# Softmax tiles of the second attention: half of TensorE's transposes go to VectorE and DMA strips, and the k projections to another PSUM bank

## The reference

```python
q = (hidden_states @ Wq).reshape(B, S, H, dh)     # k and v alike
scores = jnp.einsum('bqhd,bkhd->bhqk', q, k) * scale + position_bias
probs = jax.nn.softmax(scores, axis=-1)
ctx = jnp.einsum('bhqk,bkhd->bqhd', probs, v).reshape(B, S, H * dh)
attn_output = ctx @ Wo
```

## Time and profile before

| | us |
|---|---|
| median of 3 runs | 1679.59 |
| lowest and highest | 1674.07, 1686.88 |
| the profiled execution | 1677.58 |
| its span | 1675.9 |
| busy in the span: PE, DVE, ACT, POOL | 1346.1, 879.9, 923.5, 522.0 |

### The profile page before, as it was taken

How to read it: one execution, slowest core, us unless ns; L and a number is a source line. 1 busy time by engine, 2 the same in 40 slices (tenths; PEclk the granted TensorE clock), 3 DMA queues, 4 the chain that set the end, 5 groups by cost and what they waited for, 6 DMA issues and landing times. The chain is left out here.

```text
span 1675.9 us, 22605 instructions
## 1 busy us (share of the span) xinstructions
PE 1346.1 (80%) x6711; PEld 596.6 (36%) x6711; DVE 879.9 (53%) x2700; ACT 923.5 (55%) x1844; POOL 522.0 (31%) x789
## 2 busy tenths in 40 slices
PE   2388988887629179999999999999999999997374
PEld 1123333332117023343343343343433433432253
DVE  2445556553311046657667657667577576674211
ACT  0277777776404047656666656666566666564031
POOL 4100222222224413233423433422433334224235
PEclk9699999999859679999999999999999999998687
DMA  3335555556129213333323333323333232333062
GB/s 71 82 83 124 114 117 116 114 119 127 22 76 310 27 41 100 96 87 111 94 82 108 108 94 109 105 78 97 94 108 95 74 107 84 91 101 95 7 153 24
DMA packets 126889, 161.22 MB, mean 96 GB/s; under 512 B 36414, under 2 KB 80909, under 8 KB 126768
## 3 DMA queue, kind: packets, MB, share of 16 engines
q1 hardware_dynamic: 99376, 119.80, 27.5%
q0 software_dynamic: 27392, 39.98, 10.6%
HBM read 61.75 MB, written 36.09 MB: 58 GB/s over the span
## 5 line engine op out<-in xcount | busy, mean ns | idle before, releaser
L1247 POOL DMA_DIRECT2D crossed<-blocks x512 | 252.3, 501 | 609.4 <-DVE blocks L1514 543.8
L1503 DVE CUSTOM_DVE_ANT_0 tile<-s_ps,bias 128x512 f32<-128x512 f32 x512 | 331.2, 684 | 79.7 <-PE s_ps L1313 49.2
L1431 ACT ACTIVATE tile<-tile,low 128x512 f32<-128x512 f32 x512 | 363.2, 715 | 2.2 <-DVE low L1503 2.2
L632 ACT ACTIVATE probs_a<-score_ps,gbound 128x1024 f32<-128x1024 f32 x256 | 268.3, 1114 | 134.2 <-PE score_ps L861 134.1
L1423 ACT ACTIVATE pT<-p_ps 128x512 f32<-128x512 f32 x256 | 152.3, 595 | 269.0 <-PE p_ps L1321 267.3
L1313 PE MATMUL s_ps<-kT,qT 64*128 64x512 f32 x1024 | 255.1, 616 | 0.0
L1336 PE MATMUL o_psb<-pT,v_b 128*64 128x512 f32 x512 | 237.0, 606 | 6.8 <-DMA crossed<-blocks 6.8
L1336 PE MATMUL o_psb<-crossed,v_b 128*64 128x512 f32 x512 | 237.0, 606 | 0.0
L1321 PE MATMUL p_ps<-ident,tile 128*128 128x128 f32 x1024 | 164.6, 283 | 23.0 <-ACT pT L1423 22.9
L1321 PEld LDWEIGHTS p_ps<-ident,tile 128*128 128x128 f32 x1024 | 107.2, 140 | 207.9 <-issue 110.8
L1514 DVE STREAM_TRANSPOSE blocks<-tile 128x512 f32<-128x512 f32 x256 | 180.9, 707 | 0.3 <-ACT tile L1431 0.3
(11 more groups left out here) (153 smaller groups left out, 1484.9 us busy)
## 6 DMA issues: line engine op xcount, KB each, us to landing
crossed<-blocks SPq DMA_DIRECT2D x512, 64.0 KB, 2.6
crossed<-blocks POOLq DMA_DIRECT2D x512, 64.0 KB, 2.4
inv_row<-inv_rows SPq DMA_DIRECT2D x128, 128.0 KB, 2.9
k_stack<-k_parts SPq DMA_DIRECT2D x96, 96.0 KB
q_stack<-q_parts SPq DMA_DIRECT2D x96, 96.0 KB
bias_skew<-bias_rows SPq DMA_DIRECT2D x8, 1024.0 KB, 12.5
w_f<-in_w SPq DMA_DIRECT2D x32, 256.0 KB, 5.5
bias<-bias_skew SPq DMA_DIRECT2D x16, 448.0 KB, 12.4
```

Source lines behind the costliest of these rows:

```text
L632: nc.scalar.activation(probs[q % 2][:, c % 4, :], score_ps[c % 2][:, :], ACT.Exp, bias=gbound[:, :]).then_inc(p_ready.sem, 1)
L1247: pool.dma_start(strip_to(n, a, m), strip_from(n, a, m)).then_inc(crossed_sw[n % 2], 16)
L1431: nc.scalar.activation(tile[k % RING][s][:, :], tile[k % RING][s][:, :], ACT.Exp, bias=low[n % 2][:, s, i:i + 1], scale=-1.0, accum_out=su ...
L1503: nc.vector.tensor_tensor_reduce(out=tile[k % RING][s][:, :], in0=s_ps[k % 2][s][:, :], in1=bias[:, h, off:off + S], scale=1.0, scalar=3.0e38,
```

## The change

Of the eight (tile, head) combinations of a pair, head 1's four went by DVE before; now head 0's tiles i = 0 and 2 do as well, and only i = 1 and 3 are turned by TensorE. `turn` and `copy_pT` thus run for odd k alone, in part 1 of a step, and `block` has two transposes for even k and one for odd k. `blocks` and `crossed` hold WIDTH = 6 columns of blocks for 4, and a strip has 3 KB on each partition for 2 KB; the number of strips is the same.

`values` has for each key tile the 512-column matmul of head 1 and two matmuls of 256 columns for head 0: first all four key tiles for the queries of tiles 0 and 2 (from `crossed`), then all four for 1 and 3 (from `pT`).

The k projection goes into `r_ps`. What used `r_ps` alone gets waits against it: the output, the router's three matmuls, and the k projections of pairs 0, 3, 5 and 6. `ROUTE` puts logits, shift, exps and picks one step later.

To have room in SBUF, RING is 3 for 4 (a tile's buffer is used again three tiles later), `pT` is half as large, and the router's turned rows share the buffer `xn`, with waits in `norm_rows` and before the router's copy.

```diff
-        HELD, RING, BLK = 3, 4, 32
+        HELD, RING, BLK = 3, 3, 32
         STRIPS = P // BLK
+        WIDTH = TB + TB // 2
...
-        pT = [sb(f"pT{n}", [P, TB, S]) for n in two]
-        blocks = [sb(f"blocks{n}", [P, STRIPS, TB, TB, BLK]) for n in two]
-        crossed = [sb(f"crossed{n}", [P, STRIPS, TB, TB, BLK]) for n in two]
+        pT = [sb(f"pT{n}", [P, TB, TB // 2, P]) for n in two]
+        blocks = [sb(f"blocks{n}", [P, STRIPS, TB, WIDTH, BLK]) for n in two]
+        crossed = [sb(f"crossed{n}", [P, STRIPS, TB, WIDTH, BLK]) for n in two]
...
-        r = Router(nc, g, sb, sem, 1, x_ring, HELD)
+        r = Router(nc, g, sb, sem, 1, x_ring, HELD, xn[:, :, :].rearrange("p t d -> p (t d)"))
...
-        pT_ps, pT_ready = Signal(sem("pT_ps"), NS), Signal(sem("pT_ready"), NS)
-        blocked = Signal(sem("blocked"), NS)
+        pT_ps, pT_ready = Signal(sem("pT_ps"), NS // 2), Signal(sem("pT_ready"), NS // 2)
+        blocked = Signal(sem("blocked"), PAIRS * WIDTH)
...
-        ROUTE = dict(stats=20, rows=22, turn=(23, 1), copy=23, logits=(24, 1), shift=24,
-                     exps=25, pick=26, runs=28, counts=(29, 1), take=29, address=30)
+        ROUTE = dict(stats=20, rows=22, turn=(23, 1), copy=23, logits=(25, 1), shift=25,
+                     exps=26, pick=27, runs=28, counts=(29, 1), take=29, address=30)
...
+        def alternate(t, odd):
+            return t[own(0), :].rearrange("p (i o q) -> p i o q", o=2, q=P)[:, :, odd, :]
+
+        def strips(n, kt):
+            return crossed[n % 2][:, :, kt, :, :].rearrange("p a i j -> p i a j")
...
-                wait(sp, blocked, b, TB * (n + 1))
+                wait(sp, blocked, b, WIDTH * (n + 1))
...
-                wait(pool, blocked, b, TB * (n + 1))
+                wait(pool, blocked, b, WIDTH * (n + 1))
...
-                    wait(pe, qk_ready, b, {1: 2, 3: 4, 4: 6, 5: 8, 6: 10, 7: 12}.get(m, 2))
+                    wait(pe, qk_ready, b, {3: 3, 4: 5, 5: 7, 6: 9, 7: 11}.get(m, 1))
...
             def project(b, n, part):
-                if part == 1:
-                    wait(pe, qk_ready, b, 2 * n + 1)
+                if part == 0:
+                    wait(pe, v_ready, b, {0: 1, 1: 3, 2: 4, 3: 5, 4: 6, 5: 7, 6: 8, 7: 8}[n])
+                    since(pe, qk_ready, b, 2 * n - 1)
                 else:
-                    wait(pe, v_ready, b, {0: 1, 1: 3, 2: 4, 3: 5, 4: 6, 5: 7, 6: 8, 7: 8}[n])
                     since(pe, qk_ready, b, 2 * n)
-                nc.tensor.matmul(m_ps[:, :], (wq, wk)[part][:, n * P:(n + 1) * P], xT[:, :],
+                    if n == 0 and b >= 2:
+                        wait(pe, r.step, b - 2, r.PLACE)
+                    if n == 3 and b >= 1:
+                        wait(pe, res_done, b - 1, 1)
+                    if n in (5, 6) and b >= 1:
+                        wait(pe, r.step, b - 1, {5: r.TURNED, 6: r.SHIFTED}[n])
+                nc.tensor.matmul((m_ps, r_ps)[part][:, :], (wq, wk)[part][:, n * P:(n + 1) * P], xT[:, :],
                                  start=True, stop=True).then_inc(qk_ps.sem, 1)
...
-                since(pe, pT_ready, b, k)
+                since(pe, pT_ready, b, k // 2)
                 for kt in range(TB):
                     last = nc.tensor.transpose(p_ps[:, kt * P:(kt + 1) * P],
-                                               tile[k % RING][0][:, kt * P:(kt + 1) * P], g["ident"][:, :])
+                                               tile[(b * NS + k) % RING][0][:, kt * P:(kt + 1) * P], g["ident"][:, :])
                 last.then_inc(pT_ps.sem, 1)
...
-                wait(pe, pT_ready, b, TB * (n + 1))
+                wait(pe, pT_ready, b, TB // 2 * (n + 1))
                 await_crossing(pe, b, n, 1)
+                h = 2 * n
                 for kt in range(TB):
-                    moved = (pT[n % 2][:, kt, :].rearrange("p (i a j) -> p i a j", i=TB, j=BLK),
-                             crossed[n % 2][:, :, kt, :, :].rearrange("p a i j -> p i a j"))
-                    for s in two:
-                        h = 2 * n + s
-                        last = nc.tensor.matmul(o_ps[own(s), :], v[:, kt, h * DH:(h + 1) * DH], moved[s],
-                                                start=(kt == 0), stop=(kt == TB - 1), skip_group_check=True)
+                    last = nc.tensor.matmul(o_ps[own(1), :], v[:, kt, (h + 1) * DH:(h + 2) * DH], strips(n, kt)[:, 0:TB, :, :],
+                                            start=(kt == 0), stop=(kt == TB - 1), skip_group_check=True)
+                    odd = kt // 2
+                    for c in (2 * (kt % 2), 2 * (kt % 2) + 1):
+                        part = pT[n % 2][:, c, :, :] if odd else strips(n, c)[:, TB:WIDTH, :, :]
+                        last = nc.tensor.matmul(alternate(o_ps, odd), v[:, c, h * DH:(h + 1) * DH], part,
+                                                start=(c == 0), stop=(c == TB - 1), skip_group_check=True)
                 last.then_inc(av_done.sem, 1)
...
-                if b >= 1:
+                if b + 1 < B:
+                    wait(pe, qk_ready, b + 1, 6)
+                else:
                     wait(pe, r.step, b - 1, r.PLACE)
...
-                        if 0 <= d - 1 < ND:
+                        if 0 <= d - 1 < ND and part == 1:
                             turn(e, 2 * (d - 1) + part)
...
             def routing(b, d, part):
                 if (d, part) == ROUTE["turn"]:
-                    r.turn(pe, b, turned, lambda: wait(pe, res_done, b, 1))
+                    r.turn(pe, b, turned, lambda: wait(pe, qk_ready, b + 1, 10) if b + 1 < B else wait(pe, res_done, b, 1))
                 elif (d, part) == ROUTE["logits"]:
-                    r.logits(pe, b, logits, lambda: None)
+                    r.logits(pe, b, logits, lambda: wait(pe, qk_ready, b + 1, 12) if b + 1 < B else None)
                 elif (d, part) == ROUTE["counts"]:
-                    r.counts(pe, b, counts, lambda: None)
+                    r.counts(pe, b, counts, lambda: wait(pe, qk_ready, b + 1, 16) if b + 1 < B else None)
...
-                nc.scalar.activation((qT, kT)[part][n % 2][:, :], m_ps[:, :], ACT.Copy,
+                nc.scalar.activation((qT, kT)[part][n % 2][:, :], (m_ps, r_ps)[part][:, :], ACT.Copy,
                                      scale=(-1.0 / math.sqrt(DH), 1.0)[part]).then_inc(qk_ready.sem, 1)
...
             def copy_pT(b, k):
                 n, i = k // TB, k % TB
-                if i == 0:
+                if i == 1:
                     since(act, av_done, b, n - 1)
-                wait(act, pT_ps, b, k + 1)
-                nc.scalar.activation(pT[n % 2][:, :, i * P:(i + 1) * P], p_ps[:, :].rearrange("p (c q) -> p c q", c=TB),
+                wait(act, pT_ps, b, k // 2 + 1)
+                nc.scalar.activation(pT[n % 2][:, :, i // 2, :], p_ps[:, :].rearrange("p (c q) -> p c q", c=TB),
                                      ACT.Copy).then_inc(pT_ready.sem, 1)
...
-                        if 0 <= d - 1 < ND:
+                        if 0 <= d - 1 < ND and part == 1:
                             copy_pT(e, 2 * (d - 1) + part)
...
             def norm_rows(b):
                 wait(dve, xT_ps, 0, b)
+                if b >= 2:
+                    wait(dve, r.logit_ps, b - 2, 1)
                 wait(dve, ln.rstd, b, 1)
...
+            def freed(b, k, s):
+
+                n, i = k // TB, k % TB
+                if s == 0 and i % 2 == 1:
+                    since(dve, pT_ps, b, k // 2 + 1)
+                else:
+                    since(dve, blocked, b, WIDTH * n + (0, 2, 3, 5)[i] + (1 + s if i % 2 == 0 else 1))
+
             def lowest(b, k, s):
                 n, i = k // TB, k % TB
                 h, off = 2 * n + s, (TB - 1 - i) * P
-                since(dve, (pT_ps, blocked)[s], b, k - RING + 1)
+                freed(b, k - RING, s)
                 if s == 0:
                     wait(dve, s_ready, b, k + 1)
                 dve.sem_inc(g["passed"], 1)
-                nc.vector.tensor_tensor_reduce(out=tile[k % RING][s][:, :], in0=s_ps[k % 2][s][:, :],
+                nc.vector.tensor_tensor_reduce(out=tile[(b * NS + k) % RING][s][:, :], in0=s_ps[k % 2][s][:, :],
...
                 if i == 0 and b * PAIRS + n >= 2:
                     await_crossing(dve, b, n, 0)
                 wait(dve, p_ready, b, 2 * k + 2)
-                nc.vector.transpose(blocks[n % 2][:, :, :, i, :].rearrange("p m c j -> p c m j"), tile[k % RING][1][:, :]).then_inc(blocked.sem, 1)
+                for s, at in ((0, TB + i // 2), (1, i)):
+                    if s == 1 or i % 2 == 0:
+                        nc.vector.transpose(blocks[n % 2][:, :, :, at, :].rearrange("p m c j -> p c m j"),
+                                            tile[(b * NS + k) % RING][s][:, :]).then_inc(blocked.sem, 1)
```

9 lines of the change are left out of this document (5 added, 4 removed).

## The result

| | before | after |
|---|---|---|
| median, us | 1678.3 | 1601.0 |
| lowest and highest | 1674.1, 1686.9 | 1597.0, 1604.3 |
| ratio, 95% interval | | 0.953 (0.949 to 0.958) |
| the profiled execution's span | 1675.9 | 1602.6 |

The change gains 77 us, 4.7%. All of it lies in the second attention. First the windows of the profile after: from the first transposition of normed rows to the last value matmul, and from 612 us. Columns as in the earlier trace rows.

The account below looks back on a forecast made before the run. TensorE's queue was taken to bound the second attention, 936 of 1675.9 us. Gross 124.6 us less 29, 19, 7 and 2 gave 67.6 us gained, from 1677.6 to 1610 us; range 1566 to 1668.

Parts of the forecast that it names:

- (a): On TensorE 128 of 256 turns go, at 0.49 us each: 62.7 us gained.
- (b): The k projection, in `r_ps`, no longer waits for ACT's copy of q: 64 x 0.61 = 39.0 us gained.
- (c): With one turn in a step, TensorE's wait for ACT's copy of `pT` goes: 22.9 us gained.
- (d): TensorE's value matmuls, four long and eight short in a pair, add 0 us; ends 0 and 220 us.
- Rival A: TensorE starts no matmul ahead of an earlier one, so value blocks cost 54 us more: 1664 us; chance 0.11.
- rival B: Array halves overlap only when passes pair one to one; value blocks cost 110 us more: 1705 us; chance 0.08.
- (e): 128 more DVE transposes between the pairs of `lowest` make TensorE's scores wait for `s_ps`: 29 us lost.
- (f): Router and norm work on DVE collides, making it some 2.7 us late at step 14, 7 times: 19 us lost.
- (g): The crossing with 96 KB strips takes about 8 us, hidden except for pair 7: 7 us lost.
- rival C: The crossing takes 11 us and the values wait 1.3 us in most pairs: 1653 us; chance 0.09.
- D: DVE in series: exps or `lowest` late by another 0.7 us in every pair, 45 us: 1655 us; chance 0.05.
- (h): At the end, one transpose and a longer crossing: 2 us lost.

Follow-up runs that it names:

- k_bank: The kernel before with only the k projection moved to `r_ps`, its waits and the router's later places; ratio 0.964 to the kernel before.
- long_first: The changed kernel with all four long value matmuls ahead of the eight short ones; ratio 1.005 to the kernel before, 87 us slower than the changed kernel.
- two_first: The changed kernel with two of an odd step's DVE transposes made ahead of `finish` and the first `lowest`; ratio 0.944 to the kernel before.
- three_first: The changed kernel with all three of an odd step's DVE transposes made ahead of `finish` and the first `lowest`; ratio 0.948 to the kernel before.

## Why the prediction was right

The time, 1601 us for 1610, lies in the range and the likeliest case came about, with a gain of 77 us for 67.6. By its steps:

(a), (b) and (c), what is removed. Both waits are gone, and 124.6 us gross look right when the new waits are added to the net: 77.9 + 24.4 (lowest) + 12.2 (crossing, 19.0 less 6.8) + 7.1 (xT, 10.4 less 3.3) + 2.8 (exp) = 124.4. But the lowered clock, some 5 x 1.7 = 8.5 us, isn't in this, so the removed work was worth some 8 us more than its terms. That the two cancel is luck. k_bank, with 45 to 61 us for the 39.0 of (b), says that a part of the 8 lies there; the rest these runs don't place.

(d), the value block at 0: right to 0.01 us (3.60 for 3.59). Rival A, strict order in TensorE, would have made the block some 0.86 us longer, and rival B 1.7. The reason given, that each pass frees its own half, is too wide: long_first shows that a pass overtakes three of the other half, and no more. The kernel's order needs less. B's limit, slower from 4.5 us a block, was some 0.7 low: at 5.37 the time is 9 us above before.

(e), the wait for the lowest: 24.4 us for 29. The longest, 1.20 us once in a batch, stands behind step 11 (before 1001.31), where 1.7 was predicted, and two_first and three_first show its cause.

(f), bursts on DVE: the place (pair 4-5) and the size were right, the mechanism half. Batch 0 has no router of a batch before it, so it shows this pair without the burst: 14.80 us before, 12.33 now, a gain of 2.5 us. In batches 1 to 6 the pair takes 15.0 us before and 15.1 now. So the burst takes back 2.5 us a batch for the 2.7 predicted, 15 us in these six for 19 in seven. But the path isn't DVE late at the values. It goes by ACT's copy of xT, queued behind an exp that waits for the late lowest (7.1 us more than before), and then by the clock (four of the five falls, 6.8 us). "What a later DVE does to ACT" was named as a risk, and costed at nothing.

(g), the crossing: 9.5 us for my 8, within the bounds 7.4 and 11. From 64 and 128 KB landing in a share of 0.55 I took 2.75 us for 96 KB; it was 3.6, since 16 strips side by side now fill the DMA engines at 0.90. It was still hidden, with 0.7 us left of the 9.7 less 8 I counted on. Of rival C's 45 waits 10 came. The last of the stage is 8.2 us for 6.8 before, the other nine have 10.8 us for my 7. The Trainium skill (DMA: Bandwidth & Descriptors, "Anatomy of one DMA") gives one DMA issued by GpSimd about 2.0 us plus its bytes at 436 GB/s, that is 0.08 us more for 96 KB than for 64. The trace disagrees where sixteen are under way at once: GpSimd's land 1.2 us later (3.6 for 2.4).

D did not come: DVE's wait for the values fell from 185.0 to 93.1 us, near the 80 that the forecast named. E did not either, as both waits are gone. (h), the end, was 4.2 us for 2: 1.4 more for the last crossing and 2.8 for an exp. Of (i) no wait shows. "Clock 1.00 throughout" was wrong.

So the 10 us by which the sum fell short are, roughly, 8 of removed work, 5 of (e) and 4 of (f), less what (g) and (h) took in excess: no one term has them.

## What to carry over

When the bounding engine gets work taken off, list for every step who is now last, by the length of each wait's queue and not by its engine's busy share: here three margins (0.6 us of DVE's order, 6 us of the crossing, an exp ahead of a copy) shrank at once, and removing one gave its gain to the next until all three were moved. Where two column halves of the array have unequal matmuls, write them alternately, one long beside its two short ones; grouped by kind they cost this kernel the whole gain. An idle stretch of TensorE in a dense stage should be costed at its length, and once more, here by 1.6 us, where the granted clock in the windows behind it is 0.50; one has to look, since of equal stretches some had it and some not.
